# A decoder layer on one core: batches by quarters, one fixed table of 64 steps in place of two looped phases

## The reference, cut to what matters

```python
# stage 1: attention, 16 query heads on 4 key/value groups, head width 128
q, k, v = x @ Wq.T, x @ Wk.T, x @ Wv.T
q = q * cos + rotate_half(q) * sin          # and k likewise
attn = softmax(q @ k.T / sqrt(128))         # 128 tokens: the window masks nothing
x = layernorm(x + (attn @ v) @ Wo.T)
# stage 2: gated long convolution, 16 heads of width 8, over ctx
kv = einsum('bhil,bhjl->bijhl', ctx, ctx)   # products of pairs of channels
y = causal_conv(kv, ssm_kernel) + kv * D    # written with an FFT
x = layernorm(x + einsum('bijhl,bhil->bjhl', y, x))
# stage 3: attention with one shared key/value head, chosen by a gate per token
gating = softmax(x @ W_gate.T)              # 16 choices, top one kept
k, v = the chosen head's slice of x @ W_qkv.T, v times its gate
att = softmax(causal(q @ k.T / 4)); x = layernorm(x + att @ v)
```

## Time and profile before

| | us |
|---|---|
| median of the runs shown | 390.02 |
| lowest and highest | 377.93, 399.72 |
| the profiled execution's span | 376.8 |
| TensorE busy in it | 336.2 (89%) |
| VectorE busy | 277.0 (74%) |
| ScalarE busy | 226.7 (60%) |
| GpSimd busy | 208.0 (55%) |

### The profile page before, as it was taken

How to read it: one execution, slowest core, us unless ns; L and a number is a source line. 1 busy time by engine, 2 the same in 40 slices (tenths; PEclk the granted TensorE clock), 3 DMA queues, 4 the chain that set the end, 5 groups by cost and what they waited for, 6 DMA issues and landing times.

```text
span 376.8 us, 6563 instructions
## 1 busy us (share of the span) xinstructions
PE 336.2 (89%) x1912; PEld 260.4 (69%) x1912; DVE 277.0 (74%) x535; ACT 226.7 (60%) x703; POOL 208.0 (55%) x291
## 2 busy tenths in 40 slices
PE   1858999999999999999999998757999999999993
PEld 1656778788778788688688686443576777667683
DVE  2765966946957947957947849986899999977752
ACT  4637567566576566567566565124568668668671
POOL 0578634855825845825846815967776677502200
PEclk9969999999999999999999999995899999899996
DMA  8901000031000031000040000000000000000000
GB/s 258 359 23 57 3 29 2 0 114 56 0 28 0 0 111 56 0 28 0 0 121 0 2 1 2 0 1 1 0 3 16 0 14 14 1 14 17 0 16 28
DMA packets 5747, 12.92 MB, mean 34 GB/s; under 512 B 992, under 2 KB 3168, under 8 KB 5472
## 3 DMA queue, kind: packets, MB, share of 16 engines
q1 hardware_dynamic: 5184, 11.90, 9.5%
q10 hardware_dynamic: 544, 0.79, 0.7%
HBM read 11.63 MB, written 1.05 MB: 34 GB/s over the span
## 4 chain that ended last, share of the span: by engine, by line
PE 36%; issue 26%; DVE 20%; POOL 11%; DMA 2%; ACT 2%; SPq 1%; POOLq 1%; DVEq 0%; ACTq 0%
PE bank L481 6%; POOL t_sin L1418 5%; PE bank L360 4%; PE bank L391 4%; POOL kv L1408 3%; PE bank L377 3%; PE bank L587 3%; PE bank L640 3%; PE bank L470 3%; POOL prob L1439 3%; DVE kv_shared L1278 2%; DMA anti<-in_anti 2%; PE bank L620 2%; DVE neg_max L1291 2%; PE bank L459 2%
## 5 line engine op out<-in xcount | busy, mean ns | idle before, releaser
L1439 POOL TENSOR_TENSOR prob<-prob,rden 128x512 f32<-128x512 f32 x32 | 33.5, 1046 | 72.2 <-DVE rden L1060 72.2
L1418 POOL TENSOR_TENSOR t_sin<-rot,sin 128x512 f32<-128x512 f32 x40 | 54.3, 1358 | 26.8 <-ACT rot L756 23.9
L780 ACT ACTIVATE prob<-bank,neg_max 128x128 f32<-128x128 f32 x128 | 45.3, 367 | 39.2 <-DVE neg_max L1053 39.1
L916 ACT ACTIVATE prob<-bank,neg_max 128x128 f32<-128x128 f32 x128 | 36.5, 369 | 15.6 <-DVE neg_max L1291 15.2
L360 PE MATMUL bank<-x_hi,w_hi 128*128 128x512 f32 x96 | 36.4, 461 | 8.6 <-ACT w_hi L737 8.1
L391 PEld LDWEIGHTS bank<-k_rope,q_rope 128*128 128x128 f32 x256 | 35.0, 200 | 10.6 <-DVE q_rope L1013 5.1
L481 PE MATMUL bank<-wo_hi,head_hi 128*128 (+1 forms) x128 | 39.0, 304 | 3.3 <-DVE head_lo L1087 3.0
L391 PE MATMUL bank<-k_rope,q_rope 128*128 128x128 f32 x256 | 35.6, 284 | 4.7 <-DVE q_rope L1013 4.7
L303 POOL TENSOR_TENSOR q_rope<-y,rot 128x128 f32<-128x128 f32 (+7 forms) x60 | 31.1, 524 | 9.9 <-ACT rot L866 9.9
L1502 POOL TENSOR_TENSOR rstd<-var_eps,half_pow 128x1 f32<-128x1 f32 (+1 forms) x18 | 12.0, 667 | 44.2 <-DVE var_eps L1207 43.2
L481 PE MATMUL bank<-wo_lo,head_hi 128*128 (+1 forms) x128 | 36.0, 282 | 0.0
(11 more groups left out here) (107 smaller groups left out, 819.4 us busy)
## 6 DMA issues: line engine op xcount, KB each, us to landing
w_raw<-in_wqkv SPq DMA_DIRECT2D x3, 768.0 KB, 5.5
toep<-in_toep SPq DMA_DIRECT2D x8, 256.0 KB, 3.0
wo_raw<-in_wo SPq DMA_DIRECT2D x4, 512.0 KB, 3.5
x_raw<-in_xt SPq DMA_DIRECT2D x2, 512.0 KB, 5.9
ctxT<-in_ctx SPq DMA_DIRECT2D x1, 1024.0 KB, 9.0
x<-in_x SPq DMA_DIRECT2D x1, 1024.0 KB, 9.9
out<-x SPq DMA_DIRECT2D x8, 128.0 KB, 1.7
wf<-in_wf SPq DMA_DIRECT2D x1, 784.0 KB, 4.3
```

Source lines behind the costliest of these rows:

```text
L780: last = act.activation(prob[:, k % 2, h * P:(h + 1) * P], score_bank[k % 2][:, h * P:(h + 1) * P], ACT.Exp, bias=neg_max[:, k % 2, h:h + ...
L916: last = act.activation(prob[:, c % 2, h * P:(h + 1) * P], fscore_bank[c % 2][:, h * P:(h + 1) * P], ACT.Exp, bias=neg_max[:, c % 2, h:h + 1])
L1418: pool.tensor_tensor(t_sin[:, par, :].rearrange("p (b t) -> p b t", b=BH), rot[:, par, :].rearrange("p (b t) -> p b t", b=BH), sin[:, :].u ...
L1439: pool.tensor_tensor(own, own, rden[:, k % 2, :].unsqueeze(2).to_broadcast([P, HG, P]), ALU.mult).then_inc(norm_done, 1)
```

## The change

The kernel is written anew around a table of 64 slots, made in Python ahead of the program.

- A quarter is two batches (256 tokens). A unit is one quarter with two groups: 8 units, four steps each, so still 32 attention steps. A projection item holds both groups side by side: 12 matmuls over 256 columns in place of 6 over 512. Q, K and O weights and their low parts are all kept on chip; they come in 20 pieces of 256 KB through a ring of four staging buffers. (The kernel before also loads each weight once.)
- V comes out with tokens on partitions (x is the stationary operand), so it needs no turning: `v_turn` and the copy vT are gone.
- The four groups of a batch are summed in the accumulation bank; `accumulate` runs 8 times over 256 columns in place of 16 times over 512.
- `SLOTS` names the step of each slot: slots 0 to 13 are attention steps A0 to A13, then F (stage 3) steps alternate with A steps until A31 in slot 48 and F17 in slot 49; slots 50 to 63 are F18 to F31. `placed(t, where)` says which other items stand in slot t at its places 1, 2, 3. The 32 convolutions all stand in slots 0 to 7, four per slot. `place(b)` puts a batch's X1 (turn of the normed x), MX (turn of the mix), X2, GQ (gate and queries), KV and KT (turn of the shared key) a fixed number of slots after its last attention step.
- All items, those of stages 2 and 3 too, use the two banks of one ring (`ring_of`, `ring_free`).
- The products of a batch are all on GpSimd, in two parts (NEAR, FAR) in two slots. The low parts of Wo move from GpSimd to VectorE. Stage 3's second score matmul uses all 128 rows. Stage 3's values are copied out of their bank by ScalarE (`evict_values`) in each step. All rotary sums are on VectorE (`DVE_UNITS = 8`), as before, now in place.

TensorE's slot, and the items' places:

```diff
-            with eng.Fori(0, NG - 1, 1) as v:
-                unit(v, 0, True, True)
-                unit(v, 1, True, True)
...
+SLOTS = []
+for _a in range(STEPS):
+    SLOTS.append(("A", _a))
+    if _a >= F_FIRST:
+        SLOTS.append(("F", _a - F_FIRST))
+SLOTS += [("F", f) for f in range(STEPS - F_FIRST, FC * NB)]
...
+DONE_AT = [AT["A", 8 * (b // 2) + 5 + 2 * (b % 2)] + 1 for b in range(NB)]
...
+    w = DONE_AT[b]
+    if b < 2:
+        return {"X1": (w + 1, 3), "MX": (w + 4, 1), "X2": (w + 4, 3), "GQ": (w + 5, 1), "KV": (w + 5, 2),
+                "KT": (w + 6, 2)}
+    g = max(w + 6, AT["F", FC * (b - 2) + FC - 1])
+    return {"X1": (w + 1, 3), "MX": (w + 5, 1), "X2": (w + 6, 1), "GQ": (g, 2), "KV": (g, 3), "KT": (g + 2, 1)}
...
+            at = {(0, 1): "K", (0, 2): "Q0", (1, 1): "Q1", (1, 2): "Q2", (2, 1): "Q3"}.get((k, where))
...
+        if n < XH // 2 and where > 1:
+            head = 2 * n + where - 2
+            out += [("C", head, 0), ("C", head, 1)]
...
+            for t in range(NT):
+                if t + 2 < NT:
+                    scores(t + 2)
+                fills(t, 1)
+                if t + 1 < NT:
+                    turn(t + 1)
+                fills(t, 2)
+                values(t)
+                fills(t, 3)
+                if t and SLOTS[t - 1][0] == "A":
+                    output(SLOTS[t - 1][1])
```

The same slot on ScalarE (`takes` takes the items out of their banks), GpSimd, and the two matmuls that change shape:

```diff
+            for t in range(NT):
+                if t + 2 < NT:
+                    exps(t + 2)
+                takes(t, 1)
+                if t + 1 < NT and SLOTS[t + 1][0] == "F":
+                    copy_prob(t + 1)
+                takes(t, 2)
+                evict_values(t)
+                takes(t, 3)
...
+            for t in range(NT):
+                takes(t, 1)
+                if t + 2 < NT and SLOTS[t + 2][0] == "A":
+                    normalize(t + 2)
+                takes(t, 2)
+                for b in range(NB):
+                    if t == DONE_AT[b] + 1:
+                        power(0, ln1, b)
...
+                    if t == DONE_AT[b] + 2:
+                        mix_products(b, NEAR)
+                    if t == DONE_AT[b] + 3:
+                        mix_products(b, FAR)
...
-                pe.matmul(out[:, :], qf[own, j, c, :], kblock[own, j, 1, :, :], start=False, stop=False)
+                    pe.matmul(out[:, :], qf[:, b % 2, c, :], kblock[:, b % 2, 1, :, :], start=False, stop=False)
...
+                for half in range(2):
+                    cols = slice(half * P, (half + 1) * P)
+                    last = three(out[:, half * TOK:(half + 1) * TOK],
```

More of the change, by code:

```diff
@@ L382, in scores @@
-            def scores(u, j, k):
-                if k == 0:
-                    pe.wait_ge(rope_done, len(ROPED) * (u + 1))
-                if isinstance(u, int) and 4 * u + k < 2:
-                    pass
-                else:
-                    pe.wait_ge(exp_done, 4 * u + k - 1)
-                for h in range(HG):
-                    last = pe.matmul(score_bank[k % 2][:, h * P:(h + 1) * P],
-                                     q_rope[:, j, h, k * P:(k + 1) * P],
-                                     k_rope[:, j, k * P:(k + 1) * P], start=True, stop=True)
-                last.then_inc(scores_done, 1)
@@ L603, in key_turn, with kv_project @@
+                last.then_inc(item_done, 1)
+            def kv_project(b):
+                for c in range(C):
+                    last = pe.matmul(ring_of(("KV", b))[:, :], x2T[:, c * P:(c + 1) * P], wf[:, c, D:3 * D],
+                                     start=(c == 0), stop=(c == C - 1))
+                last.then_inc(item_done, 1)
             def key_turn(b):
                 pe.wait_ge(krep_done, b + 1)
-                if isinstance(b, int) and b == 0:
-                    pe.wait_ge(qf_lo_done, 1)
@@ new lines, in turn @@
+            def turn(t):
+                kind, n = SLOTS[t]
+                if kind == "A":
+                    pe.wait_ge(norm_done, n + 1)
+                else:
+                    pe.wait_ge(exp_done, t + 1)
+                if t:
+                    wait_copied(pe, t - 1)
+                for h in range(HG):
+                    last = pe.transpose(turn_bank[:, h * P:(h + 1) * P], prob[:, t % 2, h * P:(h + 1) * P],
+                                        ident[:, :])
+                last.then_inc(turn_done, 1)
@@ new lines, in takes @@
+            def takes(t, where):
+                for item in placed(t, where):
+                    take(item)
+            split_x(0)
+            split_stage(0)
+            split_stage(1)
+            rotate("K", 0)
+            split_stage(2)
+            rotate("Q0", 0)
+            split_stage(3)
+            rotate("Q1", 0)
+            split_stage(4)
+            rotate("Q2", 0)
+            split_stage(5)
+            split_stage(6)
+            rotate("Q3", 0)
+            exps(0)
+            copy_v(0, 0)
@@ new lines, in takes, with sums @@
+            def takes(t, where):
+                for item in placed(t, where):
+                    take(item)
+            def sums(t, where):
+                for item in placed(*((t, where - 1) if where > 1 else (t - 1, 3))):
+                    if item[0] in ROPED and item[1] < DVE_UNITS:
+                        add_sin(*item)
+            split_x(0)
+            split_stage(0)
+            dve.wait_ge(in_trig, 32)
+            split_stage(1)
+            take_cos("K", 0)
+            split_stage(2)
@@ L1538, in _layouts @@
+            power(2, ln3, NB - 1)
 def _layouts(a):
```

1846 lines of the change are left out of this document (784 added, 1062 removed).

## The result

The changed kernel takes **506.24 us** (505.2 to 508.08), 1.340 times the kernel before, 95% interval 1.334 to 1.347. Forecast were 429 us and a range from 355 to 475: slower was right, the size was not.

What follows compares the result with a forecast made beforehand. It took TensorE to bound both loops and the mixing's chain the passage between. 27 us start, 293 of TensorE's work, 103 of waits and 6 at the end gave 429 us; range 355 to 475.

Steps and rivals of the forecast that it cites:

- term of -12 for the 128 rows: Stage 3's second score matmul: 128 rows in place of 64 save 0.37 us in each of 32 steps, -12 us.
- sign that all three score matmuls would be 0.23 apart: Last stage on TensorE: the three score matmuls would each start 0.23 us apart, where before 0.41, 0.42 and 0.23.
- 1 ring, slots 0 to 8: Slots 0 to 7: convolutions wait for the two ring banks, 2.9 us in some slots, plus staged pieces; together 19 us.
- 2 first mixing, slots 9 to 12: First two batches' mixing: TensorE waits at X1, MX and X2 for GpSimd and the mix's sum; 24 us taken.
- 3 X1 of batches 2 to 7: TensorE waits at X1 for the norm's chain, with too little work of its own: 3 us each, 18 us.
- 4 thin pairs: Slot pairs without items: TensorE waits for attention's chain, 1.9 us six times and 1.3 three times; 13 us.
- 5 MX, X2 and others to slot 49: Slots 19 to 23, 38 and 39: MX and X2 wait behind a full VectorE, 3 us late in slot 21; 13 us.
- 6 last batch: Slots 50 to 63: some 40 us from X1 to first scores against 22 us of TensorE work; 16 us of wait.
- The clock: Rival: TensorE's clock falls in five places of 4 to 9 us of wait, +30 us, 460 us; chance 0.17.
- That the order pays: Rival: a wait lets other slots run ahead, so each wait term keeps a quarter; faster, 352 us; chance 0.23.
- rival of the busiest engine: Rival: each slot's largest engine sets it, 353 us in slots; about no change, 386 us; chance 0.14.
- Loads at nothing: Weight pieces through the ring of four: nothing charged; about 3 us for one landing if the cover is gone.

Runs made afterwards that it cites:

- e3: The kernel before with stage 3's second score matmul on 128 rows in place of 64: 375.91 us, ratio 0.992 to the kernel before.
- e2: The changed kernel with stage 3's second score matmul back to 64 rows: 516.81 us.
- e1: The changed kernel with 763 extra matmuls, whose result nothing reads, at 54 places where TensorE waits: 477.62 us.
- e8: The changed kernel with ScalarE's copies for each slot's first item moved ahead of the exponentials: 482.72 us.
- e14: The changed kernel with ScalarE's item copies first, norm steps in one piece, x split earlier, and 504 unread matmuls at 42 places of waiting: 438.34 us.
- e12: The kernel before with 128 rows in the second score matmul, plus 30 unread matmuls in the passage's one long wait: 377.41 us, ratio 0.995 to the kernel before.

## Why the prediction was wrong, and what in it was right

In short: the sum had no term for the clock, which cost 44 us, and its waits were 27 us too small, almost all of it in terms 4 and 5.

**TensorE's work: right.** Forecast 304 us by distances, found 305.5. The projections' matmuls start 0.12 us apart, as taken. The term of -12 for the 128 rows was too large: 0.29 us a step in e3 and 0.28 in e2, 9 us. The sign that all three score matmuls would be 0.23 apart came true for the second distance (0.24), for the first only behind output matmuls.

**VectorE: 20 us less, forecast 9.** One part of it is the building of `toep`, 481 ns an instruction in place of 904.

**Start: 6 us short.** Slot 0 begins at 32.8 us, forecast 27. VectorE's last step for the first turn, a reciprocal, ends at 30.6, and TensorE then waits 1.8 us for the normalization on GpSimd, which the forecast left out. **End: right,** 6.3 us for 6.

**The waits: right in their places, 27 short in the sum, 46 with the waits filled.** In slots, by my six terms (a term's wait in e1 is its pads, at 0.12 us each, and the rest):

| term | forecast | after | e1 |
|---|---|---|---|
| 1 ring, slots 0 to 8 | 19 | 21.0 | 22.5 |
| 2 first mixing, slots 9 to 12 | 24 | 26.8 | 30.8 |
| 3 X1 of batches 2 to 7 | 18 | 17.3 | 17.8 |
| 4 thin pairs | 13 | 20.8 | 27.0 |
| 5 MX, X2 and others to slot 49 | 13 | 26.8 | 28.7 |
| 6 last batch | 16 | 17.6 | 22.1 |
| sum | 103 | 130.3 | 149.0 |

In slot 9 I had 5 us for X1 and it was 7.0, in slot 10 9 and it was 7.6; starts of slots 5 and 6 were to be over 12 us apart and are 13.8. Terms 1 and 3 are right. Terms 4 and 5 failed, 26 us forecast and 47.6 found. Term 4 was added up wrong: six times 1.9 and three times 1.3 are 15.3, not 13, and the chain's addends make 4.6 us, not 4.8. Term 5 had VectorE late by 3 us at one X2; X2 is waited for 3.9 us twice (slots 23 and 39), and items wait for a bank of the ring there too, some 10 us from slot 13 on (the projections of slots 20 and 34 2.2 and 3.1 us), where term 1 had such waits in slots 0 to 6 only. Term 2's sum is right for a wrong reason: 6.8 us of it are K's wait for the low part of x in slot 12, which I had not seen. And the walk had it that the exponentials stand ahead of the rotation, but priced it as a wait at the ring; it was worth 23.5 us (e8).

**The clock: the step that failed first.** It stood as a rival ("five places of 4 to 9 us of wait", +30, chance 0.17) beside the forecast, though both have the same cause: if the waits come, the clock falls. Found are 19 stretches and 44 us, and behind waits of 0.6 and 1.8 us too. With the +30 of that rival in the sum the forecast is 459; with waits, clock and start at their found size (130.3, 44.2, 32.8) it is 506, within 2 us of the span; as the clock is counted as the rest of that span, this says only that no other large term is missing. That the clock is a cost of its own is shown by e1 and e14. The kernel before had it on a smaller scale: 38.9 us of waits with 9.2 of clock.

**The rivals.** That the order pays (0.23) asked for under 57 us of waits in slots, and found 130. The rival of the busiest engine asked for queues that always have work ready and gave the slots 353 us; they took 465. The range was said to end at the cases' bounds, but a quarter more of waits gives 455, the clock's case 460, and it ended at 475. Neither case has both, and both came.

**Loads at nothing: right.** No wait of TensorE in slots 1 to 63 is for a transfer.

## What to carry to other kernels

- If a forecast is made of waits, the clock belongs into the same sum: in these kernels 3 to 4 us of wait went with about 1 us added by the clock. Filling the waits with unread matmuls gave back two thirds of it or more (28.6 us of 44, 20.7 of 27). It gave nothing where one chain of the other engines set the time (e12).
- Look in each slot for the engine whose first instruction waits for two others, and give it what is ready: one call moved on ScalarE was worth 23.5 us, a move of the turn that was seen waiting longest 4.7.
- I would judge a rearranged loop by whether each engine always has something ready that waits for no one in the same slot; the loop before had a piece of attention between any two items, and 97%. This is a reading, not a result: no run puts attention between the items of the new slot, or gives the ring a third bank.

## What the runs showed that I had not expected

- Waits of 0.6 and 1.8 us in 4.2 us are followed by 3.4 us at the lower clock, while one of 0.8 us in each unit of the loop before is not.
- At half clock the output matmuls of 256 columns start 0.21 us apart, for 0.12 at full clock: less than double.
- How far the first 512-column fp32r score matmul of stage 3 starts ahead of the second depends in the changed kernel on what stands before it. At full clock it is 0.23 us behind output matmuls, 0.32 behind turns of x and behind the last stage's values, and 0.63 behind a 512-column float32 matmul such as attention's values. In that last case it starts only 0.03 us after the matmul ahead, where a values matmul otherwise takes 0.43, and 0.03 + 0.63 is 0.43 + 0.23: what looks like its own price is the rest of the matmul ahead.
